# Three key and value buffers, and each round of attention scores read by two engines, in a four-layer cross-attention network

## The chip, the cores and the metric

The kernel runs on one core of one Trainium2 chip. The metric is the time on the device in microseconds (us), the median of several runs; lower is better. The input is x, 4 batches of 1024 rows of 256, with a context of 4 batches of 154 rows of 256. All data are fp32 unless a line says bf16.

## The reference, cut to what matters

Four layers follow one another. Each has a gated cross-attention of 16 heads of 16 (in layer 0 of 32 features, made by exp(z) and exp(-z)) over the 154 context rows, and then a gated feed-forward of its own kind.

```python
x = x + tanh(g_xattn[l]) * xattn_l(layernorm(x), ctx, ctx, ...)    # l = 0..3
x = x + tanh(g_ffn[l])   * ffn_l(layernorm(x), ...)

# xattn, layers 1 to 3 (layer 1 has a mask by batch, layer 3 a mask by query row and key)
scores = einsum('bhqd,bhkd->bhqk', q, k) / sqrt(16)
attn = softmax(where(mask == 0, low, scores), axis=-1)
out = einsum('bhqk,bhkd->bhqd', attn, v) @ Wo + bo
# ffn: 0 butterfly layers with gelu, 1 linear with two of eight low-rank experts,
#      2 ternary weights with gelu, 3 silu(h1) * h3 with two of eight low-rank experts
```

## The kernel before

**Streams.** Four streams (s.i from 0 to 3) each own 256 rows of a batch and go through its four layers; then they load their rows of the next batch. So there are 4 x 4 x 4 = 64 attentions and as many feed-forwards. The engines share one PSUM tensor `P` of eight banks. Banks 0 to 3 are `quad`, which holds one round of scores or of scores on their way to the exponential; banks 4 to 7 are handed out one by one.

**Keys and values.** For each batch and layer stream 0 has `key` and `val` made once for all streams. Keys land in `KB[(4b + l) % 2]`, four groups of 154 columns, and values in `VB` and `VR`. ACT's `key` waits (`s.d_o`) until all streams are through the attention two places back. POOL then scales (layer 0, L880) or masks (layer 1, L883) the keys and copies the last 26 of the 154 columns into a tile `KT` of 32 columns (L886), since the tail of 26 keys is treated apart from the first 128. After layer 2's key POOL writes the columns of ones into `VB[0]` and `VR[0]` again (`sums`), because layer 0 had overwritten them.

**One attention.** After the projection (`qp`) come four rounds, two halves of the rows (i) by two groups of heads (u). In each, `sc` on PE writes scores for 128 rows into the four banks of `quad`, 2 x 154 columns in each (L1176 in layer 0, L1192 and L1195 in layers 1 and 2, L1184 and L1188 in layer 3), and `mx` on DVE reduces all 1232 columns to eight maxima in one instruction (L1911). The next `sc` or `s2` waits for that (`quad_free`). After the fourth round POOL's `split` cuts the maxima into three bf16 parts, `mt` turns them, and the scores are computed once more with keys along the partitions and the maximum taken off: `st` (layer 0, L1222 and L1224) or `sts` (other layers, L1251 and L1254) for the tail, in two banks, and `s2` (L1275, L1278) for the first 128 keys, in `quad`. `ex` on ACT takes the exponential of 2048 columns into the tile `ET` (L1659), `pv` multiplies with the values (L1288, L1295), `no` and `nz` divide by the sums, and `out` (L1360) projects and adds.

**Order.** Each engine has a list of stages, written before the kernel is built. The generator `turns` says per stream which stage follows which. `orders` picks for each engine in turn the stream that the string `TURN` names by a digit, with costs from `parts` (nanoseconds by stage) and tokens for what is shared: one token for `quad`, one for `ET`, one for each free bank. Where it expects PE to stand for over 450 ns it writes `fill` into PE's list: matmuls on an identity (L1011) whose result nobody reads. On the chip all waits are semaphores and each engine takes its list in order.

Of the kernel before, what the change touches and what calls it, by code (L numbers as in the profile page):

```python
# [29 lines left out]
def build(nc, d, out):  # L30
# [5 lines left out]
    with ctx:  # L36
# [15 lines left out]
        zc = sb("zc", [128, 1])  # L52
# [11 lines left out]
        ctxT = [sb(f"ctx{i}", [128, 2, NP]) for i in range(2)]  # L64
# [37 lines left out]
        mk = sb("mk", [128, 4, NK], bf16)  # L102
# [8 lines left out]
        KB = [sb(f"KB{i}", [128, 4, NK]) for i in range(2)]  # L111
        KT = [sb(f"KT{i}", [128, 4, 32]) for i in range(2)]
        VB = [sb(f"VB{i}", [128, 16, 32]) for i in range(2)]
        VR = [sb(f"VR{i}", [128, 4, 32]) for i in range(2)]
# [29 lines left out]
        l_ctx = [sem(f"l_ctx{i}") for i in range(2)]  # L144
# [22 lines left out]
        g_one = sem("g_one")  # L167
# [3 lines left out]
        q_d = sem("q_d")  # L171
        q_a = sem("q_a")
# [4 lines left out]
        for i in range(NS):  # L177
# [8 lines left out]
            s.sm = sb(f"sm{i}", [128, 16, 4])  # L186
            s.g8 = sb(f"g8_{i}", [128, 6, 2, 8])
            s.mx = sb(f"mx{i}", [128, 2, 4, 4])
            s.z = sb(f"z{i}", [128, 32])
# [44 lines left out]

            s.Et = s.Et[:]
# [25 lines left out]
        def parts(name, of):  # L261
# [6 lines left out]
                  "sts": 1451 if name == "sts" and of[2] == 3 else 1113, "s2": (1105, 1105, 1105, 1540)[l],  # L268
# [4 lines left out]
                   "val": 460 if name == "val" and of[1] == 0 else 610, "norm": 885, "mx": 1357, "pv": 700, "no": 950 if l == 0 else 1240, "nz": 1655, "out": 700,  # L273
# [6 lines left out]
                   "h1": 275, "h2": 275, "norm": 985, "no": 580}  # L280
            pool = {"split": 1460 if l == 3 else 1100, "key": 2040 if name == "key" and of[1] == 0 else 1400, "mw": 1650, "norm": 1515, "sq": 960,
# [4 lines left out]
                   "key": "PA" if name == "key" and of[1:] == [0, 0] else "PAG" if name == "key"  # L286
                   else "PA", "val": "PDA" if name == "val" and of[1] == 0 else "PD", "norm": "DGA", "bias": "g",
# [11 lines left out]
        SHAPES = {"sc": "bb", "s2": "bb", "sts": "dd", "st": "ee", "lin": "bb", "tl": "hh", "val": "af", "fill": "aa"}  # L299

        def shapes(name, of):

            if name == "sts" and of[2] == 3:
                return "cd"
# [15 lines left out]
        def takes(name, of, engine):  # L320
            if (name, engine) in (("sc", "PE"), ("s2", "PE")):
                return ["quad"]
# [10 lines left out]
        def gives(name, of, engine):  # L333
            if (name, engine) in (("mx", "DVE"), ("ex", "ACT")):
                return ["quad"]
# [60 lines left out]
        def turns(s):  # L396
# [35 lines left out]
            for b in range(4):  # L432
                for l in range(4):
                    if s.i == 0:
                        if (b, l) == (0, 1):
                            yield "after", "masks"
                        if 4 * b + l >= 2:
                            for s_ in S[1:]:
                                yield "after", ("attention", s_.i, 4 * b + l - 2)
                        yield "name", "free"  # L440
# [4 lines left out]
                        yield "need", "free"  # L445
# [148 lines left out]
                "0323032023232332002022021201220221000331030331331032121212012121020321202302321203221323013213300332"  # L594
                "1310320201201203203121310310021002011321013210203231230220022013231030303311332030120121312020010320"
                "2102121313023113213200202030132321312013101003030233030232012120120103001010031303213132102112100121"
                "0231023032302000303200030030013020031000000022031032210131211111011211111112111211111330113021020230"
                "2202121023212212202222222130200222210012211032303133231232333233333333333333321230302322122032030231"
                "0321300312132330102033103021013123130100320021021321130113102032313020220220321310303033210133031201"
                "2010021200310212323121102313120103200220313221210130131003003323303020321201202101300101003130321231"  # L600
                "2130121100121021302303230003200200001000300003003000320230101230122321010031211110111111111111111113"
                "3211321202020320221210222122212222122210200222200322302310311311232323332303332333332333233333221330"
                "3221230303213031301201303312330102030201231020313100310202310213211311021230301302022022032131030303"
                "3210133031202121020031020210132312110321312010230022031222310130130110320330323023203012021101030100"
                "1303033130121120121120102120213023032300231030300031013000030000000002022030322101213011011211111111"
                "1111111112133211032102020320122102202221222012002122222222231001223123031301332312333333323333332333"
                "3332123030232212233032310103203120320331233010102030121031231031012012003023211301131020323130202202"
                "2032131030230133133032021012102003102021013232111021112330202201232030312313110103230300302232302030"
                "2101010130001130033103123112012121012102103230230230032003003030103000000032000010022100322321013121"
                "1112111111111111111112133113212232222222222222222222222332232333333333333333333333333333",  # L610
            "ACT":
                "0000300312211232020023003323101122112030103031202212201213133033103201202312231233032002021101310031"
                "3302022102102010331331213212200022021301313310323012230012100020130133020302111312201010310320223213"
                "0101023201320331000330300000021001000022313211213110111111211211211130003202012232112232222222203002"
                "2210011033132303212333333333333301202232203203102110212013230301323131123303200202313011310031303022"
                "2021102001333132112310020202230231131301033212203012100020103133020302111312201010130322202313010102"
                "3210230313033000000003100000020121321231020130110110111111111121323220221221212222222220002223030033"
                "1311212013233333303333323332312220323030110211203133013230021322131303002320231301113031030022202110"
                "2003313131212321200022023301131301302312200213010200130323021030111312101300312023022312101020212033"
# [1687 lines left out]
```

## Time and profile before

| what | value |
|---|---|
| median of 3 runs | 2433.03 us (2433.03 to 2433.96) |
| span of the profiled execution | 2431.5 us |
| time of the profiled execution beside its span | not recorded; its span is 1.5 us under the median |
| PE busy | 2331.2 us (96%), of which filler 138.0 us |
| DVE busy | 1274.5 us (52%) |
| ACT busy | 1140.6 us (47%) |
| POOL busy | 853.3 us (35%) |
| maxima, L1911 | 256 times, mean 1435 ns, 367.3 us |
| DMA | 39.28 MB, 16 GB/s on average |

Engines: PE is TensorE, DVE VectorE, ACT ScalarE, POOL GpSimd, SP SyncE, and PEld the loading of weights, which overlaps PE. An fp32 matmul stands in the trace as two records.

### The profile page before, as it was taken

To read this page: it belongs to the slowest core of one execution; us is meant where nothing else is said; L and a number is where in the kernel's file an instruction comes from. 1 tells how busy PE (TensorE), PEld (TensorE's weight loads), DVE (VectorE), ACT (ScalarE), POOL (GpSimd) and SP (SyncE) were. 2 spreads that over 40 slices of the span, in tenths; PEclk is the share of its full clock that TensorE was granted. 3 is DMA by queue.
4 is the path that set the end of the run, shared out by engine and by line. 5 is a ranking of instruction groups with operands and counts; after the bars stand their busy time and mean duration, and the time that the engine had idled before them with its cause. 6 is when DMAs were issued, how large, how long until landed. Compare 5 with 4: busy or idle time off the path is not lost.

```text
span 2431.5 us, 56000 instructions
## 1 busy us (share of the span) xinstructions
PE 2331.2 (96%) x23735; PEld 1578.7 (65%) x23735; DVE 1274.5 (52%) x2833; ACT 1140.6 (47%) x1762; POOL 853.3 (35%) x1546
## 2 busy tenths in 40 slices
PE   8999989999999999999999999899999999899999
PEld 5676545777776655577777655467777765457777
DVE  6544776545433567644442467764544346765442
ACT  5545487323345558632225546752333455683211
POOL 1232333434331333334432232334434223334342
PEclk9999999999999999999999999999999999999999
DMA  3200120000000000000000000000000000000000
GB/s 141 91 13 2 35 101 2 1 10 10 10 22 1 13 1 16 2 10 10 10 1 21 1 13 1 13 2 10 10 10 10 13 2 13 2 2 2 1 9 9
DMA packets 17462, 39.28 MB, mean 16 GB/s; under 512 B 1792, under 2 KB 11840, under 8 KB 16192
## 3 DMA queue, kind: packets, MB, share of 16 engines
q1 hardware_dynamic: 17216, 35.71, 4.3%
q8 instruction: 190, 3.11, 0.5%
q14 instruction: 56, 0.46, 0.1%
HBM read 29.78 MB, written 4.19 MB: 14 GB/s over the span
## 4 chain that ended last, share of the span: by engine, by line
PE 79%; ACT 7%; DVE 7%; issue 4%; POOL 2%; DMA 0%; ACTq 0%; POOLq 0%; DVEq 0%
PE P L1501 9%; PE P L1288 5%; PE P L1360 5%; PE P L1385 5%; PE P L1510 5%; PE P L1534 5%; PE P L1502 5%; PE P L1372 4%; PE P L1519 4%; PE P L1278 4%; ACT ET L1659 3%; PE P L1295 3%; PE P L1195 3%; PE P L1140 3%; DVE mx L1911 3%
## 5 line engine op out<-in xcount | busy, mean ns | idle before, releaser
L1911 DVE TENSOR_REDUCE mx<-P 128x8 f32<-128x1232 f32 x256 | 367.3, 1435 | 199.2 <-PE P L1195 119.9
L1501 PE MATMUL P<-Et,w 128*128 128x256 f32 x1024 | 265.4, 382 | 0.1
L1501 PEld LDWEIGHTS P<-Et,w 128*128 128x128 f32 x1024 | 191.5, 190 | 63.2 <-issue 34.5
L1955 DVE SCALAR_TENSOR_TENSOR x<-P,w_first,x 128x512 f32<-128x512 f32 x96 | 71.8, 749 | 277.6 <-PE P L1385 96.8
L1613 ACT ACTIVATE Et<-x,sm 128x256 f32<-128x256 f32 x256 | 138.7, 592 | 138.5 <-POOL sm L906 138.1
L1659 ACT ACTIVATE ET<-P 128x2048 f32<-128x2048 f32 x96 | 180.2, 1877 | 43.3 <-PE P L1278 39.9
L1737 ACT ACTIVATE gu<-P 128x256 f32<-128x256 f32 x128 | 49.1, 384 | 307.1 <-PE P L1502 290.4
L2120 DVE SCALAR_TENSOR_TENSOR gu<-gu,P 128x256 f32<-128x256 f32 x128 | 53.8, 420 | 230.0 <-ACT gu L1737 229.9
L900 POOL TENSOR_SCALAR sm<-mv 128x2 f32<-128x2 f32 x96 | 18.6, 194 | 413.5 <-DVE mv L1906 411.5
L1278 PE MATMUL P<-R,KB 32*128 32x256 f32 (+1 forms) x2560 | 155.3, 379 | 0.0
L1288 PE MATMUL P<-ET,VB 128*32 128x256 f32 x2048 | 143.4, 385 | 11.3 <-ACT ET L1659 5.3
L1502 PE MATMUL P<-gu,b 128*128 128x256 f32 x512 | 152.3, 379 | 0.0
L924 POOL TENSOR_TENSOR x<-x,w_bias 128x512 f32<-128x512 f32 x112 | 142.0, 1271 | 21.3 <-ACT Et L1613 21.1
L1011 PE MATMUL P<-identb 128*128 128x512 bf16 x507 | 138.0, 385 | 7.7 <-POOL mg L873 4.5
L953 POOL TENSOR_TENSOR R<-R 128x512 f32<-128x512 f32 x48 | 61.1, 1273 | 233.1 <-DVE R L1947 233.0
L1510 PE MATMUL P<-gu,b 128*128 128x256 f32 x512 | 134.5, 385 | 0.1
L977 POOL TENSOR_TENSOR Et<-Et,gu 128x512 f32<-128x512 f32 x48 | 61.0, 1271 | 179.0 <-DVE Et L2127 178.9
L1372 PE MATMUL P<-Et,wup 128*128 128x256 f32 x512 | 123.7, 386 | 0.0
L1534 PE MATMUL P<-w_w,R 128*128 128x256 f32 x512 | 116.4, 380 | 0.4 <-DVE R L2143 0.4
L1385 PE MATMUL P<-wdn,R 128*128 128x256 f32 x512 | 114.4, 381 | 0.0
L1510 PEld LDWEIGHTS P<-gu,b 128*128 128x128 f32 x512 | 94.1, 190 | 23.3 <-DVE gu L2127 7.7
L1372 PEld LDWEIGHTS P<-Et,wup 128*128 128x128 f32 x512 | 93.3, 190 | 24.2 <-issue 12.3
(287 smaller groups left out, 4971.3 us busy)
## 6 DMA issues: line engine op xcount, KB each, us to landing
kvw<-in_wkv SPq DMA_DIRECT2D x12, 672.0 KB, 4.1
x<-in_x SPq DMA_DIRECT2D x16, 256.0 KB, 2.7
out<-x SPq DMA_DIRECT2D x16, 256.0 KB, 2.1
w<-in_w SPq DMA_DIRECT2D x2, 1024.0 KB, 6.6
w<-in_wexp SPq DMA_DIRECT2D x1, 1028.0 KB, 9.2
w_w<-in_wcon SPq DMA_DIRECT2D x1, 1024.0 KB, 11.4
w_w<-in_m3t SPq DMA_DIRECT2D x1, 1024.0 KB, 7.2
w<-in_w1q SPq DMA_DIRECT2D x1, 1024.0 KB, 10.5
```

What stands on the lines that cost most here:

```text
L924: e.tensor_tensor(s.x[:], s.x[:], gb[:, k:k + 1, :].broadcast_to([128, 2, 256]), ALU.add).then_inc(s.g_x, 1)
L1278: t = e.matmul(quad[h, g, cols], K[G4[g], j, h], s.QT[G4[g], j if l == 0 else u, :], start=False, stop=True, skip_group_check=True)
L1288: t = e.matmul(o[G4[q], :], of(q), ET[:, g, 256 * a:256 * a + 256], start=start, stop=False, skip_group_check=True)
L1372: t = e.matmul(o[:, 256 * (j % 2):256 * (j % 2) + 256], wup[:, c, 128 * j:128 * j + 128], s.xT[:, c, :], start=c == 0, stop=c == 1)
L1385: t = e.matmul(o[:, 256 * i:256 * i + 256], s.hT[:, j, 128 * i:128 * i + 128], wdn[:, j, :], start=j == 0, stop=j == 7)
L1501: e.matmul(o, wm[:, c, js], s.xT[:, c, :], start=n == c == 0, stop=False, skip_group_check=True)
L1502: t = e.matmul(o, bm[:, js], U[:, 2 * n, :], start=False, stop=False, skip_group_check=True)
L1510: t = e.matmul(P[:, k, 256 * n:256 * n + 256], bm[:, js], U[:, 2 * n + 1, :], start=False, stop=n == 1, skip_group_check=True)
L1534: e.matmul(o, s.G[:, j, rows], w2[:, j, :], start=j == 0, stop=False)
L1613: e.activation(s.xn[:, i, :], s.x[:, i, :], ACT.Identity, bias=s.sm[:, 6, i:i + 1], scale=s.sm[:, 2, i:i + 1]).then_inc(s.a_xn, 1)
L1659: e.activation(ET[:].rearrange("p g c -> p (g c)"), quad.rearrange("p g c -> p (g c)"), ACT.Exp, bias=mb1[:, b:b + 1] if l == 1 else 0.0). ...
L1911: e.tensor_reduce(s.mx[:, i, :, 2 * u:2 * u + 2], quad[:, :, 0:2 * NK].rearrange("p g (a k) -> p g a k", a=2), AX.X, ALU.max).then_inc(q_d, 1)
```

## The change

1. Three buffers of keys instead of two (`kb`), each 160 columns wide with zeros from column 154 on, so that the tail is read from the key tile itself and `KT` goes. ACT's `key` waits for the attention three places back. Of three value buffers number 0 belongs to layer 0, the other two take turns (`vb`), so `sums` is not repeated. To make room, `ctxT` has one buffer (its next load follows layer 3's `val`), the mask of layer 1 is made for one batch at a time on POOL, and some small tiles are shared.
2. `mx` reduces banks 0 and 1 alone. A new stage `mc` on ACT copies banks 2 and 3 to SBUF (`s.half`), and `my` on DVE takes their maxima there. `quad` has two tokens, one given by `mx` and one by `mc`; `sc` and `s2` take both.
3. `sts` reads tail keys that lie apart, so its stationary tiles are 32 columns wide instead of 64, twice as many.
4. The strings `TURN` are new for all engines.

```diff
-        KB = [sb(f"KB{i}", [128, 4, NK]) for i in range(2)]
-        KT = [sb(f"KT{i}", [128, 4, 32]) for i in range(2)]
...
+        KB = [sb(f"KB{i}", [128, 4, NP]) for i in range(3)]
+        VB = [sb(f"VB{i}", [128, 16, 32]) for i in range(3)]
+        VR = [sb(f"VR{i}", [128, 4, 32]) for i in range(3)]
+
+        def kb(b, l):
+            return KB[(4 * b + l) % 3]
+
+        def vb(b, l):
+            n = 1 + (3 * b + l - 1) % 2 if l else 0
+            return VB[n], VR[n]
...
+            s.half = [w.rearrange("p (g a k) -> p g a k", g=2, a=2) for w in (R[:, 1024:1640], s.Et[:].rearrange("p a b -> p (a b)")[:, 0:616])]
...
-                        if 4 * b + l >= 2:
+                        if 4 * b + l >= 3:
                             for s_ in S[1:]:
-                                yield "after", ("attention", s_.i, 4 * b + l - 2)
+                                yield "after", ("attention", s_.i, 4 * b + l - 3)
...
                             yield "sc", s, b, l, i, u
+                            yield "name", "sc"
                             yield "mx", s, i, u
+                            yield "need", "sc"
+                            yield "mc", s, i, u
+                            yield "my", s, i, u
...
-                if l == 3 and b < 2:
+                if l == 3 and b < 3:
                     e.wait_ge(p_v0, 4 * b + 4)
-                    load_ctx(b + 2)
+                    load_ctx(b + 1)
...
-                if u == 0 and 4 * b + l >= 2:
+                if u == 0 and 4 * b + l >= 3:
                     for s in S:
-                        e.wait_ge(s.d_o, 2 * (4 * b + l - 1))
+                        e.wait_ge(s.d_o, 2 * (4 * b + l - 2))
...
+            def mc(s, i, u):
+                n = C.up(s.p_s)
+                e.wait_ge(s.p_s, n)
+                if i:
+                    e.wait_ge(d_top, tops[s.i][n - 3])
+                e.activation(s.half[u], quad[:, 2:4, 0:2 * NK].rearrange("p g (a k) -> p g a k", a=2), ACT.Copy).then_inc(q_a, 1)
...
             def mx(s, i, u):
                 e.wait_ge(s.p_s, C.up(s.p_s))
-                e.tensor_reduce(s.mx[:, i, :, 2 * u:2 * u + 2],
-                                quad[:, :, 0:2 * NK].rearrange("p g (a k) -> p g a k", a=2), AX.X, ALU.max).then_inc(q_d, 1)
-                C.up(q_d)
+                e.tensor_reduce(s.mx[:, i, 0:2, 2 * u:2 * u + 2],
+                                quad[:, 0:2, 0:2 * NK].rearrange("p g (a k) -> p g a k", a=2), AX.X, ALU.max).then_inc(q_d, 1)
+
+            def my(s, i, u):
+                e.wait_ge(q_a, copied[s.i][C.at(s.p_s) - 1])
+                e.tensor_reduce(s.mx[:, i, 2:4, 2 * u:2 * u + 2], s.half[u], AX.X, ALU.max).then_inc(d_top, 1)
```

## Rows read from the trace of the kernel before

**Rows 1.** The page: span, busy time by engine, engines of the last chain.

```profile
span 2431.5 us, 56000 instructions
PE 2331.2 (96%) x23735; PEld 1578.7 (65%) x23735; DVE 1274.5 (52%) x2833; ACT 1140.6 (47%) x1762; POOL 853.3 (35%) x1546
...
PE 79%; ACT 7%; DVE 7%; issue 4%; POOL 2%; DMA 0%; ACTq 0%; POOLq 0%; DVEq 0%
```

**Rows 2.** Windows: length, busy PE, PEld, DVE, ACT, POOL, clock, DMA; four mixed summed.

```profile
sum 912.00, PE 838.68 PEld 493.19 DVE 607.47 ACT 583.97 POOL 310.40; mean PE 209.67 PEld 123.30 DVE 151.87 ACT 145.99 POOL 77.60
...
425.60:790.40 364.80, 362.96 (x3331) 265.32 (x3328) 158.56 (x344) 132.59 (x234) 134.11 (x214) 1.00 0.03 9
...
912.00:972.80 60.80, 56.37 (x761) 30.98 (x754) 45.59 (x94) 52.31 (x66) 20.77 (x47) 1.00 0.05 16
```

**Rows 3.** Windows of filler line L1011 alone (PE, PEld): four mixed summed, start.

```profile
sum 912.00, PE 103.35 PEld 34.01; mean PE 25.84 PEld 8.50
...
0.00:60.80 60.80, 14.95 (x52) 5.46 (x53) 0.97 0.38 141
```

**Rows 4.** Waits of PE: us in total, times, longest.

```profile
PE P L1195 <- ACT ET L1659: 6.8, 17, 0.9
PE P L1184 <- DVE mx L1911: 6.7, 17, 0.8
PE P L1288 <- ACT ET L1659: 5.3, 9, 2.0
PE P L1288 <- issue: 4.7, 14, 0.5
...
PE P L1275 <- DVE mx L1911: 3.8, 10, 0.6
...
PE P L1195 <- DVE mx L1911: 3.5, 8, 0.6
...
PE P L1176 <- ACT ET L1659: 1.6, 4, 0.6
```

**Rows 5.** Timeline of a layer-3 attention: start, us, what.

```profile
951.24 0.70 PE L1188 MATMUL P<-KB,R 32*64 32x308 f32 x16
...
952.13 1.43 DVE L1911 TENSOR_REDUCE mx<-P 128x8 f32<-128x1232 f32 x1
...
953.62 0.31 PE L1184 MATMUL P<-mb,identb 32*64 32x308 bf16 x1 [0.27 <-DVE mx L1911]
```

**Rows 6.** Groups by line: busy us, mean ns, idle before; maxima and tail matmuls.

```profile
L1911 DVE TENSOR_REDUCE mx<-P 128x8 f32<-128x1232 f32 x256 | 367.3, 1435 | 199.2 <-PE P L1195 119.9
...
L1254 PE MATMUL P<-R,KT 32*64 32x256 f32 x768 | 56.0, 379 | 0.0
...
L1251 PE MATMUL P<-R,selt 32*64 32x256 bf16 x384 | 28.3, 280 | 3.7 <-ACT R L1640 2.5 <-issue 0.8 <-ACT R L1679 0.2
...
L1224 PE MATMUL P<-R,KT 32*32 32x256 f32 x512 | 20.3, 376 | 0.0
...
L1222 PE MATMUL P<-R,selt 32*32 32x256 bf16 x256 | 9.5, 273 | 0.8 <-ACT R L1640 0.8
```

**Rows 7.** Nearest reduction and ACT copies from PSUM; the third row by source.

```profile
L2038 DVE TENSOR_REDUCE sm<-Et 128x2 f32<-128x512 f32 x16 | 10.9, 682 | 22.8 <-ACT Et L1613 22.7
...
L1622 ACT ACTIVATE Et<-P 128x512 f32<-128x512 f32 x96 | 56.9, 595 | 97.6 <-PE P L1116 97.3
...
L1667 ACT ACTIVATE R<-P x49: 360/384/600, 56.0 to 1942.8; 128x256 f32<-128x256 f32 x34, 128x512 f32<-128x512 f32 x15
```

**Rows 8.** Windows of L1911 alone, first and last of the four mixed stretches.

```profile
182.40:425.60 243.20, 51.38 (x36) 1.00 0.11 35
...
2006.40:2188.80 182.40, 39.49 (x28) 0.99 0.02 5
```

**Rows 9.** Waits of ACT: keys.

```profile
ACT KB L1595 <- PE P L1084: 1.3, 2, 1.1
```

**Rows 10.** DMA issues: KB each, median us to landing.

```profile
ctx<-in_ctx SPq DMA_DIRECT2D x4, 160.0 KB, 3.9
```

More of the change, by code:

```diff
@@ L62, in res @@
             return W[name]
-        ctxT = [sb(f"ctx{i}", [128, 2, NP]) for i in range(2)]
+        ctxT = sb("ctxT", [128, 2, NP])
         first = res("first", [128, 467])
@@ L143, in build @@
         l_last = sem("l_last")
-        l_ctx = [sem(f"l_ctx{i}") for i in range(2)]
+        l_ctx = sem("l_ctx")
         FIRST = ("first",)
@@ L333, in gives @@
         def gives(name, of, engine):
-            if (name, engine) in (("mx", "DVE"), ("ex", "ACT")):
-                return ["quad"]
+            if (name, engine) in (("mx", "DVE"), ("mc", "ACT"), ("ex", "ACT")):
+                return ["quad"] * (2 if name == "ex" else 1)
             if (name, engine) == ("pv", "PE"):
@@ L444, in turns @@
                         yield "name", "key"
-                        yield "need", "free"
+                        yield "need", "begun"
+                        if 3 * b + l >= 3:
+                            n = 3 * b + l - 3
+                            before = 4 * (n // 3) + n % 3 + 1 if l else 4 * (b - 1)
+                            for s_ in S[1:]:
+                                yield "after", ("attention", s_.i, before)
                         yield "val", b, l
@@ L599, in build @@
[L599 to L603, printed above, removed]
@@ L762, in build @@
         ORDER = orders()
+        tops = [[n for n, of in enumerate((of for of in ORDER["DVE"] if of[0] == "my"), 1) if of[1] is s] for s in S]
+        copied = [[n for n, of in enumerate((of for of in ORDER["PE"] if of[0] in ("sc", "s2")), 1)
+                   if of[0] == "sc" and of[1] is s] for s in S]
         def sp_program(e):
@@ L929, in split @@
                 parts_ = s.MX.rearrange("p i (g r) -> p (i g) r", r=32)
-                e.wait_ge(q_d, [n for n, of in enumerate((of for of in ORDER["DVE"] if of[0] == "mx"), 1)
-                                if of[1] is s][16 * b + 4 * l + 3])
+                e.wait_ge(d_top, tops[s.i][16 * b + 4 * l + 3])
                 e.wait_ge(s.g_z, C.at(s.g_z))
@@ L1248, in sts @@
                 for u in range(2):
-                    o = [banks[g // 2][64 * h:64 * h + 64, 256 * u:256 * u + 256] for g, h in enumerate((0, 1, 1, 0))]
-                    for g in range(4):
-                        e.matmul(o[g], selt[G4[g], 2 * u:2 * u + 2, :].rearrange("p a k -> p (a k)"), s.MT[G4[g], :],
-                                 start=l < 3 and u == 0, stop=False, skip_group_check=True)
-                    for g in range(4):
-                        t = e.matmul(o[g], K[G4[g], u, :], s.QT[G4[g], u, :], start=False, stop=True, skip_group_check=True)
+                    eight = [(g, a, banks[g // 2][G4[2 * h + a], 256 * u:256 * u + 256]) for a in range(2)
+                             for g, h in enumerate((0, 1, 1, 0))]
+                    for g, a, o in eight:
+                        e.matmul(o, selt[G4[g], 2 * u + a, :], s.MT[G4[g], :], start=l < 3 and u == 0, stop=False,
+                                 skip_group_check=True)
+                    for g, a, o in eight:
+                        t = e.matmul(o, K[G4[g], 2 * u + a, :], s.QT[G4[g], u, :], start=False, stop=True,
+                                     skip_group_check=True)
                 t.then_inc(s.p_q, 1)
```

209 lines of the change are left out of this document (101 added, 108 removed).

## Prediction

> **What bounds the kernel now.** I read the page first. TensorE is busy for 96% of the span and carries 79% of the chain that ended last [rows 1]. This kernel's planner also writes filler matmuls into TensorE's list wherever it expects a gap, so that busy share is not all work. The windows view by stage and the same view for the filler line L1011 alone part the two. The span alternates between two kinds of stretch. In the dense ones (the last feed-forward, line L1501 and its kin) PE is busy 362.96 of 364.8 us with almost no filler, so nothing that shortens a wait can help there. The four mixed ones, with over half of the attention rounds in them (182.4 to 425.6, 790.4 to 1033.6, 1398.4 to 1641.6 and 2006.4 to 2188.8 us), sum to 912.0 us. PE is busy 838.7 us there and 103.4 of these are filler [rows 2, 3]. So idle 73.3 + filler 103.4 = 176.7 us is what a better order could win there. About 30 to 40 us more lie at the start (14.95 of filler in the first 60.8 us) and at the end, and the change hardly touches those.
>
> Next, what ends PE's waits. PE idles 2431.5 - 2331.2 = 100.3 us in all. The maxima (L1911) end 6.7 + 3.8 + 3.5 = 14.0 us of it, 14%, in 35 waits of 0.40 us on average, the longest 0.8. The exponentials (L1659) end 6.8 + 5.3 + 1.6 = 13.7 us of it, also 14% [rows 4]. The timeline of one layer-3 attention shows why: the last score matmul ends at 951.94, DVE begins its maxima at 952.13, holds all four banks of `quad` for 1.43 us, and the next round starts at 953.61 [rows 5]. One round occupies `quad` for about 2.66 us, and more than half of it is DVE's.
>
> **The change part by part, on the profiled execution's span of 2431.5 us.**
>
> The hold of `quad`. The maxima took 1435 ns for 1232 elements, and DVE's reduction of 512 took 682 [rows 6, 7]. The slope is 753 / 720 = 1.05 ns per element, so 616 elements cost 682 + 109 = 0.79 us. On ACT 512 elements cost 595 ns and 256 a median of 384, so a copy of 616 costs 0.68 us [rows 7]. Both run side by side after one handover, so the hold falls by 1435 - 790 = 0.645 us in each of the 256 rounds. The mixed stretches hold 36 + 35 + 37 + 28 = 136 rounds (the first and the last of the four windows are shown) [rows 8], and of them only what PE waited for counts. Filler hides waits in the same places, so I give the maxima their 14% of the whole 176.7 us: 24.7 us. As the mean wait (0.40) is under 0.645, most of it can go, though another wait may come last in its stead. Bounds 0 and -25 us; I take four fifths, **-20**.
>
> The length of one attention. Each attention has four rounds. The first three release `quad` 0.645 sooner, 1.9 us. The fourth now ends later for `split`, which waits for the maxima of the copied half: the two reductions in a row are at least 1.58 us and copy, handover (0.19) and reduction are 0.68 + 0.19 + 0.79 = 1.66, against 1.44, so +0.2. Net -1.7 us; a stream has 16 attentions, 27 us if its chain set the time everywhere. 136 of 256 rounds, 53%, lie in the mixed stretches: 14 us. Here the new lists belong too. They can spend the shorter hold, and the third buffer lets a key run three attentions ahead of the slowest stream instead of two. ACT's keys hardly ever waited for an old buffer: the 1.3 us they idled was for PE [rows 9]. So I give the buffer nothing by itself. Bounds 0 and -50 (a third of the 176.7 us less the first term); I take **-14**.
>
> `sts`. The tail's stationary tiles become 32 wide, so matmuls double from 16 to 32 instructions (records from 24 to 48, as an fp32 matmul has two). Before, layers 1 to 3 cost (56.0 + 28.3) / 48 = 1.76 us of PE per call, and layer 0, which already has the 32-wide form, (20.3 + 9.5) / 16 = 1.86 [rows 6]. So twice the instructions cost 0.1 us and not twice the time: 48 x 0.1 = **+5**. Bounds +3 and, if equal moving data from one row group went one after the other, 48 x 0.6 = +29; the row of layer 0 is so near in form that I stay by it. In layer 3 the form of tile now also differs from that of `s2` right behind, 16 more switches. The nearest row is PE's idle without a releaser ahead of the 128 x 32 matmuls, 4.7 / 14 = 0.34 us [rows 4]; 0 to +5, I take **+2**. The Trainium skill (TensorEngine Tiling (Array Packing), Tiling Modes, Key Properties) says that changing the tiling mode drains TensorE; by that rule a switch costs something each time. No row of this case isolates one, and without a cost the sum would be 2 us lower.
>
> ACT and DVE. The copies are 256 x 0.68 = 174 us more on ACT (1140.6 to 1315). In the mixed stretches 136 x 0.68 = 92 us come on top of 584.0, which makes 74% of 912. An ACT queue 16% fuller brings the exponentials later. Their 14% of 176.7 us is 24 us, times 0.16 is 4 us. Behind a waiting copy also stand the turns and projections of other streams, so I take **+7**. Lower bound 0. The upper one is read in the fullest window, 912.0 to 972.8 us: ACT 52.3 busy, with 8 rounds, so 8 x 0.68 = 5.4 more gives 57.7 of 60.8 us. If ACT were the limit in such a window in each of the four mixed stretches, that is +22. On DVE two halves cost 1.58 against 1.435, 256 x 0.145 = 37 us, of which 20 in the mixed stretches (607.5 to 627, 69%) [rows 2]. That is covered by the third of the time in which DVE stands idle there; without that cover it would cost the same 20 us. The Trainium skill (VectorE: DVE Perf Modes, the section on the TRN2 errata) speaks against cutting the reduction: each instruction pays a fixed cost, 120 cycles from PSUM and 58 from SBUF. An estimate by its table is 0.77 + 0.70 us for the halves against 1.41, some 16 us in all; the rows say 37, and neither is on the path.
>
> At nothing: the 16 copies to `KT` go from POOL (35% busy) and one mask per batch comes there; masking keys for layer 1 alone stays. One buffer for `ctx`: its load now begins after layer 3's `val` and takes 3.9 us [rows 10]. Layer 0's keys of the next batch come with a whole attention between, so it is hidden; uncovered it would be 3 x 3.9 = 12 us. SP stands in order, so it could sit behind a `store`, which is waited for anyway.
>
> The sum: -20 - 14 + 5 + 2 + 7 = -20, so 2411.5 us of span. The profiled span is 1.5 us under the median of the three runs (2433.03), so **2413 us**.
>
> **Rivals.**
> The lists win much more (21%). The planner's order was tied to one token for `quad`; with two halves and three buffers the dense feed-forward of one stream may lie beside the attention of others. For it: 176.7 us of slack stand in stretches where neither DVE (67%) nor ACT (64%) is full. Against it: ACT reaches 86% in some windows, and the digits of the new PE list show the same long runs of one stream in the last feed-forward. Time: all 24.7 us of the maxima, a fifth of the other 152 (30), less 14: 2433 - 41 = 2392, or down to 2375 with a third.
>
> Nothing is left (14%). `quad` is freed sooner, but the next wait is one of the other 86%, and the two gains shrink to the 14 us of cost: 2433 us. For it: the waits for the maxima are short, and PE usually has other streams' matmuls between the rounds. This also stands for the change not doing what it says.
>
> ACT becomes the limit, slower (20%). A round needs both readers, and ACT takes its list in order. A copy that stands behind an exponential of 1.88 us, or behind a table load, gives the banks back later than the old reduction did. It decides once copies come more than 1.435 - 0.68 = 0.75 us late on average. For it: ACT 95% full in the window above. Against: the lists know of the copy and place it. Price: +22 in the four full windows, +7 for `sts`, +7 of queueing elsewhere, less some 20 still won: 2433 + 16 = 2449.
>
> The forecast has 45%, with a range of its own from 2401 to 2427.
>
> **The numbers.** The measurement of this kernel tells about 0.2% (4.9 us) from no change. Faster by more: 45% + 21% + 2% of the third case = 68%. Within 0.2%: 12%. Slower: 20%. The range for 8 in 10 goes from 2378, which leaves some 5% of the large-gain case below, to 2446, which leaves about 12% above.
>
> **What the profile will show.** The maxima should have two groups of 256 at about 0.79 us, and a new ACT copy 256 times at 0.68. PE's waits for the maxima should fall from 14.0 us to under 5, some of them named after the copy. Filler and idle in the mixed stretches should go from 177 to about 150 us. The tail matmuls should cost 1.86 us a call, ACT some 1315 us and DVE 1311. The prediction fails if copies start long after the scores end, if filler stays at 138 us, or if the new lists shift so much that the mixed stretches are no longer the same ones. It also fails if the granted clock, 1.00 in most windows, falls in longer gaps.

## The result, and the profile after

The changed kernel takes 2415.53 us, the median of four runs (2414.88 to 2420.39), beside 2433.03 for the kernel before. The ratio is 0.9931, with a 95% interval from 0.9917 to 0.9945. So 17.5 us are gone, where 20 had been forecast.

The page of the profile first: the span, and the busy time of each engine. It answers to [rows 1].

```profile
span 2413.9 us, 58830 instructions
...
PE 2317.5 (96%) x24838; PEld 1578.3 (65%) x24838; DVE 1292.7 (54%) x3088; ACT 1303.3 (54%) x2026; POOL 845.0 (35%) x1522
```

ACT is busy 162.7 us longer and DVE 18.2, and PE 13.7 us less, although its tail has twice the instructions. Most of that is filler, which fell from 138.0 to 126.3 us (507 matmuls to 458). PE's idle time went from 100.3 to 2413.9 - 2317.5 = 96.4. What PE does beside filler is 2191.2 us, against 2193.2 before. Nearly the whole gain is therefore slack in PE's list, that is, idle time and filler: 238.3 us before, 222.7 after, 15.6 of the 17.6 us between the two spans. The groups of the page, by line (busy us, mean ns, idle before them and what ended most of it):

```profile
L1926 DVE TENSOR_REDUCE mx<-P 128x4 f32<-128x616 f32 x256 | 203.1, 793 | 188.5 <-PE P L1208 97.6
...
L1024 PE MATMUL P<-identb 128*128 128x512 bf16 x458 | 126.3, 390 | 15.6 <-POOL mg L895 5.6
...
L1668 ACT ACTIVATE Et<-P 128x616 f32<-128x616 f32 x128 | 87.2, 681 | 88.0 <-PE P L1208 43.9
L1668 ACT ACTIVATE R<-P 128x616 f32<-128x616 f32 x128 | 87.1, 681 | 70.3 <-PE P L1208 33.4
```

and from the same kind of groups, asked for by engine, the reductions of the copied half and the tail matmuls, which answer to [rows 6]:

```profile
L1931 DVE TENSOR_REDUCE mx<-R 128x4 f32<-128x616 f32 x128 | 100.4, 784 | 6.4 <-ACT R L1668 6.4
L1931 DVE TENSOR_REDUCE mx<-Et 128x4 f32<-128x616 f32 x128 | 100.2, 784 | 7.4 <-ACT Et L1668 7.3
...
L1265 PE MATMUL P<-R,KB 32*32 32x256 f32 x1536 | 61.7, 376 | 0.0
...
L1262 PE MATMUL P<-R,selt 32*32 32x256 bf16 x768 | 30.5, 272 | 5.0 <-ACT R L1649 4.7 <-issue 0.3
```

One reduction of 1435 ns has become one of 793 ns from PSUM and one of 784 ns from SBUF, with a copy of 681 ns on ACT beside them. These durations may not simply be added up, because one instruction starts before the one in front of it ends. Two reductions back to back in DVE's timeline (start, length, what):

```profile
943.24 0.79 DVE L1926 TENSOR_REDUCE mx<-P 128x4 f32<-128x616 f32 x1
943.94 0.79 DVE L1931 TENSOR_REDUCE mx<-Et 128x4 f32<-128x616 f32 x1
```

The second starts 0.70 us after the first, which takes 0.79. So the durations of the halves exceed those of the whole reduction by 203.1 + 200.6 - 367.3 = 36.4 us, but DVE's busy time, which counts overlap once, grows by far less: by 14.4 us against the run below that differs from the changed kernel in the halves alone (1278.3 to 1292.7).

By stage, the same four mixed stretches (slices of equal share of the span, 905.25 us in all), every engine first, then filler line L1024 alone; they answer to [rows 2, 3]:

```profile
sum 905.25, PE 838.15 PEld 506.74 DVE 599.62 ACT 623.14 POOL 300.90; mean PE 209.54 PEld 126.68 DVE 149.91 ACT 155.78 POOL 75.22
```

```profile
sum 905.25, PE 94.39 PEld 31.49; mean PE 23.60 PEld 7.87
```

Idle 67.1 and filler 94.4 make 161.5 us, where it was 176.7: 15.2 of the 17.5 us were won in the mixed stretches. The waits of PE (us in total, times, longest), which answer to [rows 4], look quite different from that:

```profile
PE P L1208 <- ACT ET L1675: 6.3, 11, 1.0
...
PE P L1197 <- DMA mbTs<-mbT: 4.7, 1, 4.7
PE P L1300 <- ACT ET L1675: 4.6, 11, 1.3
...
PE P L1024 <- DVE mx L1926: 3.9, 4, 1.6
PE P L1197 <- DVE mx L1926: 3.6, 8, 1.1
...
PE P L1208 <- DVE mx L1926: 2.8, 7, 0.9
...
PE P L1287 <- DVE mx L1926: 1.3, 4, 0.5
...
PE P L1205 <- DVE mx L1926: 1.0, 3, 0.4
...
PE P L1189 <- DVE mx L1926: 0.6, 2, 0.3
```

Maxima still end 3.9 + 3.6 + 2.8 + 1.3 + 1.0 + 0.6 = 13.2 us of PE's idle time (9.3 if those ahead of filler are left aside), hardly less than the 14.0 before; waits under the name of the copy itself (L1668) add 3.0. Whoever looked only here would say that the change had done nothing. The row `mbTs<-mbT` is new: one single wait of 4.7 us. Layer 3's first masked scores wait there for the last of the transfers that spread the mask over the partitions. In the kernel before, the last of them was issued at 305.3 us and the first scores that need it ran at 360.9; in the changed kernel it was issued at 352.4, and PE stood until 354.6. The same wait stands in the runs below that use these lists (4.0 us even with the buffers of the kernel before), so it came with the new order. The prediction has no term for it. Part of the reason for the 13.2 shows in the timeline of a late copy (start, length, what; idle before and releaser in brackets):

```profile
938.21 2.11 PE L1024 MATMUL P<-identb 128*128 128x512 bf16 x9
...
938.39 1.91 ACT L1719 ACTIVATE R<-R 128x2048 f32<-128x2048 f32 x1
...
939.17 0.79 DVE L1926 TENSOR_REDUCE mx<-P 128x4 f32<-128x616 f32 x1
940.21 0.67 ACT L1668 ACTIVATE R<-P 128x616 f32<-128x616 f32 x1
...
940.94 0.10 PEld L1197 LDWEIGHTS P<-mb,identb 32*64 32x64 bf16 x1 [1.12 <-DVE mx L1926]
940.97 0.29 PE L1197 MATMUL P<-mb,identb 32*64 32x308 bf16 x1 [0.66 <-issue]
```

DVE is through with its half at 939.96. The copy stood behind another stream's instruction of 1.91 us, ended only at 940.88, and then the next round began, at 940.94 with its weight load. The banks were held until 940.88 by ACT, 0.9 us longer than by DVE; without the split DVE would have given them back at 939.17 + 1.43 = 940.60. The bracket books the 1.12 us before that weight load to DVE's maxima, so some waits under that name are the copy's. In the timeline I paired the ends of all 256 copies and reductions: the copy ends first or within 0.1 us of the reduction in 206 rounds, more than 0.1 us later in 50, more than 0.5 us later in 31, at worst 2.8 us. What these delays add to the holds is 39 us in all, of which only a part meets a waiting PE.

One more thing moved with the slack: the clock that PE was granted. Its mean is 0.997 in the profile before and 0.999 after, of a full clock of 2.4 GHz, and the windows show why. These are the stretches at the lower of its two levels, half of it; first the four of the kernel before, then the one of the changed kernel (stretch, length, PE busy, clock, DMA share, GB/s):

```profile
38.91:42.33 3.42, 3.42 (x21) 0.50 0.00 0
1414.49:1417.90 3.41, 3.41 (x40) 0.50 0.00 0
1537.37:1540.78 3.41, 3.41 (x30) 0.50 0.03 7
2086.91:2090.32 3.41, 3.41 (x22) 0.50 0.00 0
```

```profile
352.08:358.91 6.83, 4.32 (x39) 0.50 0.78 279
```

In the 6.8 us ahead of them PE had stood idle for 1.4 to 3.0 us in the kernel before, and for 2.2 us in the changed one, whose stretch begins within the wait for the mask. If what PE did in them took twice as long as at the full clock, they cost 13.65 / 2 = 6.8 us before and 4.32 / 2 = 2.2 after. The runs say much the same: of the four of the changed kernel, three with a mean clock of 0.999 took about 2415 us and the one with 0.996 took 2420.4, so 0.002 is worth some 3.4 us. An estimate of 3 to 5 of the 17.5 us is therefore the clock. No run holds it fixed, so it can't be told apart from the shorter idle times that go with it.

### The profile page after: what moved, and what is told of

It reads as the page before. It is cut to its first block and busy times, and to the rows that moved or that the text cites. A ratio compares the mean times of both kernels' runs of the same rounds, so it can differ in the third digit from the quotient of the medians.

```text
span 2413.9 us, 58830 instructions
## 1 busy us (share of the span) xinstructions
PE 2317.5 (96%) x24838; PEld 1578.3 (65%) x24838; DVE 1292.7 (54%) x3088; ACT 1303.3 (54%) x2026; POOL 845.0 (35%) x1522
## 5 line engine op out<-in xcount | busy, mean ns | idle before, releaser
L1926 DVE TENSOR_REDUCE mx<-P 128x4 f32<-128x616 f32 x256 | 203.1, 793 | 188.5 <-PE P L1208 97.6
L938 POOL TENSOR_TENSOR x<-x,w_bias 128x512 f32<-128x512 f32 x112 | 142.2, 1273 | 11.7 <-ACT Et L1622 11.6
L1024 PE MATMUL P<-identb 128*128 128x512 bf16 x458 | 126.3, 390 | 15.6 <-POOL mg L895 5.6
L1668 ACT ACTIVATE Et<-P 128x616 f32<-128x616 f32 x128 | 87.2, 681 | 88.0 <-PE P L1208 43.9
L1668 ACT ACTIVATE R<-P 128x616 f32<-128x616 f32 x128 | 87.1, 681 | 70.3 <-PE P L1208 33.4
```

What stands on the lines that cost most here:

```text
L938: e.tensor_tensor(s.x[:], s.x[:], gb[:, k:k + 1, :].broadcast_to([128, 2, 256]), ALU.add).then_inc(s.g_x, 1)
L1668: e.activation(s.half[u], quad[:, 2:4, 0:2 * NK].rearrange("p g (a k) -> p g a k", a=2), ACT.Copy).then_inc(q_a, 1)
L1926: e.tensor_reduce(s.mx[:, i, 0:2, 2 * u:2 * u + 2], quad[:, 0:2, 0:2 * NK].rearrange("p g (a k) -> p g a k", a=2), AX.X, ALU.max).then_inc ...
```

## The experiments

Two theories went in. **A**: the shorter hold of `quad` (with lists made for it) brings the gain, the copies cost a little of it, and the third key buffer nothing. **B**: the gain comes from elsewhere, from the third buffer or from lists that are simply better searched, and the copy is free or does harm. Experiments that put new stages or a longer search to use have their own written-out lists. Filler is not in these lists; the generator places it anew for every kernel, so its amount may differ where the stages' order is the same. The twelve runs were made in three groups of four, each with its own runs of the kernel before (medians 2433.03, 2433.68 and 2433.14 us). Each ratio is taken within its group, and a difference in us between runs of different groups is no finer than about 1 us.

**The shorter hold undone.** The changed kernel and its lists, without the stages `mc` and `my`; one reduction takes all four banks again.

```
-    yield "mc", s, i, u
-    yield "my", s, i, u
...
-    e.tensor_reduce(s.mx[:, i, 0:2, 2 * u:2 * u + 2], quad[:, 0:2, 0:2 * NK]...)
+    e.tensor_reduce(s.mx[:, i, :, 2 * u:2 * u + 2], quad[:, :, 0:2 * NK]...)
```

> The changed kernel with its new lists, but one reduction of all four banks again: the ACT copies and the reductions from SBUF are taken out of the lists, every other stage stays in its order. Theory (the shorter hold of the banks, which the new lists are cut to, brings the gain): 2433 to 2442 us, that is 18 us or more above the changed kernel, and PE's waits for the maxima at 14 us or more. Rival (the new lists or the three buffers bring it, whoever reads the scores): 2412 to 2420 us, since ACT then has 174 us less to do.

Measured: 2443.54 us, ratio 1.0043 (1.0029 to 1.0058). That is 28 us above the changed kernel and 10 above the kernel before, and 1.5 above the expected range. The page, and its waits of PE:

```profile
PE 2324.4 (95%) x24836; PEld 1580.5 (65%) x24865; DVE 1278.3 (52%) x2831; ACT 1149.9 (47%) x1768; POOL 846.6 (35%) x1522
```

```profile
PE P L1279 <- DVE mx L1918: 9.2, 23, 1.2
PE P L1190 <- DVE mx L1918: 7.5, 14, 1.1
PE P L1201 <- DVE mx L1918: 7.3, 14, 1.6
...
PE P L1198 <- DVE mx L1918: 3.6, 7, 0.9
...
PE P L1272 <- DVE mx L1918: 1.4, 3, 0.6
PE P L1182 <- DVE mx L1918: 1.4, 4, 0.5
```

With the same lists and a hold of 1436 ns, the waits for maxima are 30.4 us; with 793 ns they are 13.2. Here the row does show what the hold costs, since the order is the same. Idle and filler together are 115.6 + 133.0 = 248.6 us against 222.7, so 25.9 of the 26.1 us between the two spans are slack. (Of it 6.7 us are filler that the generator placed on top, 485 matmuls against 458.) The 28 us are what the shorter hold brings after the copies and DVE's second reduction have been paid. B's part about the lists falls: the new lists without the shorter hold are worse than the old ones. They spend it, and by themselves they lose. (Of the 10 us some 4 belong to the tail and the other parts, as is shown further down, so the order itself is about 6 us worse.)

**Two key buffers.** The changed kernel with `KB` two deep, the waits set back to the attention two before.

```
-            return KB[(4 * b + l) % 3]
+            return KB[(4 * b + l) % 2]
```

> The changed kernel with its new lists, but keys in two buffers by turns, and the key stage of ACT waits for the attention two places back again. Theory (the third key buffer by itself brings nothing, because ACT hardly ever waited for an old one): 2413 to 2418 us, the same as the changed kernel. Rival (the new lists use the room of three): 2420 us or more, with idle time of ACT or PE in front of the keys.

Measured: 2415.98 us, ratio 0.9935 (0.9918 to 0.9951), against 0.9931 with three. The third key buffer brings nothing that can be measured, as the theory had it.

**The 32-wide tail in the kernel before.** Only `sts` is changed, the lists stay.

```
+    eight = [(g, a, banks[g // 2][G4[2 * h + a], 256 * u:256 * u + 256]) for a in range(2) for g, h in enumerate((0, 1, 1, 0))]
-    for g in range(4):
-        t = e.matmul(o[g], K[G4[g], u, :], s.QT[G4[g], u, :], ...)
+    for g, a, o in eight:
+        t = e.matmul(o, K[G4[g], 2 * u + a, :], s.QT[G4[g], u, :], ...)
```

> The kernel before with one edit: the tail scores of layers 1 to 3 use stationary tiles of 32 columns, twice as many matmuls. Theory (0.1 us more a call, 48 calls, most of it on the path): 2438 us, and up to 2443 if the switch of tile form in layer 3 costs as well; the tail lines at 1.86 us a call. Rival (PE fills its gaps elsewhere, so a longer call hides in idle and filler time): 2431 to 2435 us. If equal moving data went one after the other: 2460 us.

Measured: 2435.56 us, ratio 1.0011 (1.0002 to 1.0021): 2.5 us slower, with an interval from 0.5 to 5.1. That is between the rival's range (up to 2435) and the theory's 2438. The groups of its tail:

```profile
L1255 PE MATMUL P<-R,KT 32*32 32x256 f32 x1536 | 61.2, 376 | 0.0
...
L1252 PE MATMUL P<-R,selt 32*32 32x256 bf16 x768 | 29.3, 273 | 3.5 <-ACT R L1642 2.3 <-issue 0.8 <-ACT R L1681 0.2
```

That is 90.5 / 48 = 1.89 us a call against 1.76, 6.2 us more busy time in all, of which 2.5 us reach the span. The rest ran where there would have been slack.

**Twice the copy.** Two key buffers (to make room in SBUF), and behind each `mc` a second ACT copy of 616 elements, from a constant to a scrap tile that nobody reads. The lists know nothing of it.

```
+    e.activation(idle[:].rearrange("p (a k) -> p a k", a=7), ones[:, 0:88].unsqueeze(1).broadcast_to([128, 7, 88]), ACT.Copy)
```

> The changed kernel, keys in two buffers to make room, and behind each of the 256 copies ACT makes one more of the same size between tiles that nobody else uses, after the banks are given back: 174 us more on ACT (about 1478 us in all), nothing else moved. Theory (ACT's load costs by queueing, about 7 us for the first 174): 7 to 22 us above the changed kernel, 2423 to 2438 us. Rival (ACT has room and its load costs nothing): 2413 to 2419 us. Rival (ACT is about to become the limit in the mixed stretches, where it is at 77%): 2445 us or more.

Measured: 2448.58 us, ratio 1.0065 (1.0048 to 1.0081), 32.6 us above the kernel with two key buffers.

```profile
PE 2320.2 (95%) x24809; PEld 1576.1 (64%) x24838; DVE 1294.4 (53%) x3088; ACT 1452.9 (59%) x2282; POOL 847.9 (35%) x1522
...
L1675 ACT ACTIVATE idle<-ones 128x616 f32<-128x616 f32 x256 | 182.5, 713 | 0.0
```

The added copies last 182.5 us, but they overlap the copies in front of them, and ACT's busy time rose by 149.4 us (from 1303.5 with two key buffers). On an ACT that was 54% busy these cost 32.6 us of span, 0.22 us for each. It was not free at half load. The theory (7 to 22 us) was too low, and the time lies in the range of the second rival (2445 or more). That ACT is about to become the limit isn't shown by it: the lists did not know of these copies, and ACT is at 59%.

**The halves alone.** The kernel before (two buffers, `KT`, 64-wide tail, two buffers of `ctx`), with `mx`, `mc`, `my` and the changed kernel's lists; only POOL's has eight stages more.

```
 kernel before
-    mx: reduce quad[:, 0:4]                (1 stage, holds quad)
+    mx: reduce quad[:, 0:2]; mc: copy quad[:, 2:4] to s.half[u]; my: reduce s.half[u]
```

> The kernel before with its own buffers (two for keys and values, KT, two for ctx) and its own 64-wide tail tiles, and only the halves of the change: mx, mc and my, with the new kernel's lists (POOL's extra key stages put where they can first start). Theory after the first four runs (halves together with lists cut to them are the whole gain, buffers are nothing): 2412 to 2419 us. Rival (the three value buffers, the zero-padded keys or the single ctx buffer carry a part): 2421 us or more.

Measured: 2411.28 us, ratio 0.9905 (0.9888 to 0.9921). The halves with their lists gain 21.8 us by themselves. Everything else of the change together (third key buffer, value buffers, the masks, `KT` gone, the 32-wide tail, one `ctx`) takes back 4.2, which is not quite what the two intervals can tell apart (up to 0.9921 and from 0.9917).

**The old design, lists searched on.** The kernel before with only its written-out lists replaced.

> The kernel before with no edit but its lists, which were searched further from where they stood. Theory (the halves are needed, order alone gives little): 2422 us or more, that is at most 11 us under the kernel before. Rival (searching the lists anew is what pays, whoever reads the scores): 2418 us or less, near the changed kernel.

Measured: 2428.4 us, ratio 0.9977 (0.9968 to 0.9987). A better order alone, as far as this search found one, is worth 4.6 us. That is what remains of B.

**The changed kernel, lists searched on.**

> The changed kernel with no edit but its lists, searched further for the same time as in the run of the kernel before with its lists searched on. Theory (the new lists are near what this search finds, and the distance between the two designs stays over 10 us): 2408 to 2414 us. Rival (the changed kernel's order is spent): 2414 to 2418 us. Rival (an order that only looks better): 2418 or more.

Measured: 2413.89 us, ratio 0.9919 (0.9902 to 0.9935): 1.6 us less than as given, less than the intervals can tell. Its order was not held back by a lack of search of this kind.

**Twice the reduction.** The changed kernel with one more DVE reduction of 616 elements, from a constant, behind each `my`; the lists know nothing of it.

```
+    e.tensor_reduce(idle[:], ones[:, 0:88].unsqueeze(1).broadcast_to([128, 7, 88]), AX.X, ALU.max)
```

> The changed kernel, and behind each of the 256 reductions from SBUF DVE makes one more of the same size (0.79 us) from and to tiles that nobody else uses: about 200 us more on DVE (1493), nothing else moved. It answers the run in which ACT's copy was doubled (33 us for 182 us of ACT). Theory (each in-order queue that carries a stream's next step costs by its load, DVE as ACT): 20 to 40 us above the changed kernel, 2435 to 2455 us. Rival (DVE has room, as the forecast had it): 2415 to 2422 us. Rival (DVE is nearer its limit than ACT): 2460 or more.

Measured: 2465.04 us, ratio 1.0129 (1.0112 to 1.0146), 49.5 us above the changed kernel.

```profile
PE 2330.7 (95%) x24838; PEld 1579.5 (64%) x24838; DVE 1462.1 (59%) x3344; ACT 1306.8 (53%) x2026; POOL 846.8 (34%) x1522
...
L1937 DVE TENSOR_REDUCE idle<-ones 128x7 f32<-128x616 f32 x256 | 200.4, 783 | 0.0
```

Here too the added reductions overlap those in front: they last 200.4 us, and DVE's busy time rose by 169.4. That is 0.29 us of span for each us, at 54% busy before and 59% with it. The time is above the theory's range and in that of the rival who had DVE nearer its limit than ACT (2460 or more). Part of it is the clock: all four runs have a mean of 0.994. In the profile PE spent six stretches at half clock, 27.3 us:

```profile
sum 27.31, PE 24.92; mean PE 4.15
```

By the same working as above they cost 12.5 us, against 2.2 in the changed kernel, so some 10 of the 49.5 us are an effect of the gaps through the clock. By the ratio of 0.29 the 14.4 us that the halves add to DVE's busy time cost 4 us. That is an estimate, and from above, since the lists of the change do place `my`.

**No copy.** The changed kernel without `mc`: `quad` is given back by `mx`, `my` reduces a constant of the same size, and so the maxima of half of the heads are left out (the exponentials are scaled by 0.001). DVE's work stays as it is, but `my` has no copy to wait for; ACT's 174 us of copies go, and `quad` has one reader.

```
-    yield "mc", s, i, u
...
-    e.wait_ge(q_a, copied[s.i][C.at(s.p_s) - 1])
-    e.tensor_reduce(s.mx[:, i, 2:4, 2 * u:2 * u + 2], s.half[u], AX.X, ALU.max)
+    e.tensor_reduce(s.mx[:, i, 2:4, 2 * u:2 * u + 2], ones[...].broadcast_to([128, 2, 2, NK]), AX.X, ALU.max)
```

> The changed kernel without ACT's copies. Banks 2 and 3 are given back by mx, which reads banks 0 and 1 alone; my makes a reduction of the same size (616 elements) from a constant tile, so the true maxima of half the heads are left out, and the exponentials scale their input by 0.001 to stay finite. DVE's load and the hold of the banks by DVE stay, 174 us of ACT go. Theory (ACT's load costs 33 us per 182 us, as the doubled copy showed, also for the first copy): about 2384 us. Rival (the lists had placed the copies where ACT had room, so the first costs less than one more that no list knows): 2395 to 2410 us. Forecast's term for ACT (7 us): 2408.

Measured: 2403.8 us, ratio 0.9878 (0.9862 to 0.9895). The copies, placed by the lists as they are, cost 11.7 us, what `my` waits for them included. That is 0.08 us for each us of ACT's busy time (1303.3 to 1147.9), and it is the rival's case. Against the whole reduction in the same lists (2443.54) this kernel is 39.7 us faster: so much is the shorter hold worth in this order before the copies are paid, with DVE's second reduction in it. Its groups show the same reduction from PSUM as the changed kernel, and less filler, 118.7 us against 126.3 (the generator placed 436 matmuls instead of 458):

```profile
L1921 DVE TENSOR_REDUCE mx<-P 128x4 f32<-128x616 f32 x256 | 203.0, 793 | 193.6 <-PE P L1204 98.1
...
L1020 PE MATMUL P<-identb 128*128 128x512 bf16 x436 | 118.7, 387 | 11.3 <-POOL mg L891 5.6
```

**The halves alone, lists searched on.** The kernel of 2411.28 us with a longer search.

> The kernel of the run with the halves alone (buffers and tail of the kernel before), its lists searched on. Theory (halves in the old buffers need fewer matmuls for the tail, and the lists were not cut to them yet): 2399 to 2408 us. Rival (its order was spent): 2409 to 2413 us.

Measured: 2409.16 us, ratio 0.9900 (0.9884 to 0.9917). Only 2 us more; I had expected about 2399 to 2408, and the rival's range (2409 to 2413) holds. Against the old design searched on (2428.4) it is 19.2 us faster, so the gain of the halves holds when both sides have had their search.

**Halves in three of the four layers.** The kernel of 2411.28 us, but layer 2 keeps the single reduction (a stage `mq`) and makes no copy; first with the lists as they were, the lost stages struck out.

```
+    HALF = (0, 1, 3)
...
+    mq: e.tensor_reduce(s.mx[:, i, :, 2 * u:2 * u + 2], quad[:, :, 0:2 * NK]..., AX.X, ALU.max)     (layer 2)
     mx, mc, my as above                                                                             (layers 0, 1, 3)
```

> As the run with the halves alone, but in layer 2 one reduction takes all four banks again and ACT copies nothing there; the lists are the same less the stages that go. It asks which layers the halves pay in. Theory (their gain is the shorter hold less ACT's and DVE's load, and in layer 2's rounds the two are about even): 2409 to 2417 us, within 6 us of the run with the halves alone (2411.3). Rival (every layer's rounds gain alike, a quarter of 28 us): 2418 us or more.

Measured: 2412.42 us, ratio 0.9917 (0.9900 to 0.9933), against 2411.28 (0.9905) with halves everywhere. In layer 2 the 64 copies and 64 extra reductions cost as much as the shorter hold gives, as far as these intervals can tell, and the rival (2418 or more) is excluded.

**The same with lists searched on.**

> The same kernel with its lists searched on. It should be the fastest: 43 us of ACT and 9 us of DVE less than with halves in all layers, in lists that can use it. Theory: 2392 to 2402 us. Rival (layer 2 gains as the others do, once the lists are searched): no better than the halves in all layers with lists searched on.

Measured: 2402.06 us (2399.09 to 2403.08), ratio 0.9869 (0.9853 to 0.9886). This is the best version that keeps the whole computation: 31 us under the kernel before and 13.5 under the changed one, in intervals that lie apart. Against the halves in all layers searched on (2409.16) it is 7.1 us faster, and there the intervals still touch (up to 0.9886 and from 0.9884). Groups of its page:

```profile
L1948 DVE TENSOR_REDUCE mx<-P 128x4 f32<-128x616 f32 x192 | 152.1, 792 | 153.3 <-PE P L1220 72.3
...
L1036 PE MATMUL P<-identb 128*128 128x512 bf16 x424 | 116.7, 387 | 7.8 <-POOL mg L896 4.6
```

Filler is at 116.7 us and PE idle for 2400.3 - 2306.5 = 93.8, 210.5 us of slack against 222.7. ACT is busy 1263.3 us, 40 less than in the changed kernel.

## Why the prediction was right, and where its terms were not

**The net result** came from the forecast's own case: -17.5 measured, -20 forecast, well in its range from 2401 to 2427. The halves gained less than their terms (-20 - 14 + 7 = -27 forecast, -21.8 measured with the halves alone) and the rest of the change cost less (+7 forecast, +4.2 measured). The two errors have opposite signs, so the sum is better than its parts, which is luck. Some 3 to 5 us of the gain also went with PE's clock, for which the forecast had no term.

**The hold and the new lists (-20 and -14).** The mechanism was right: in one and the same order of stages, the hold of 1436 instead of 793 ns costs 28 us with the copies paid and 39.7 without them, and this stands in idle time and filler. The size of the gain before its costs can be put together: 21.8 net, 11.7 for the copies (measured in the changed kernel), and for DVE's extra work something between 0.08 and 0.29 us for each of its 14.4, that is 1 to 4. This makes 35 to 38 us, an estimate, against 34 forecast. The split of it between a first term for the wait and a second one for the length of an attention can't be measured, because an order spends the shorter hold as it likes. It stays an argument. What the shorter hold gives in the old order wasn't run.

**ACT's copies (+7).** Under-sized: 11.7 us. The lower bound of nothing is excluded, the upper of 22 is not reached. The step priced queueing ahead of the exponentials; what it left to a rival is the lateness of the copy itself, which 50 of 256 rounds show. That rival ("ACT becomes the limit") named a mechanism that is there, but not its case: it asked for copies 0.75 us late on average, and here 203 of 256 end before DVE's reduction does, while 50 are late. How the 11.7 us divide between late copies, queueing and the waits of `my` was not measured.

**DVE at nothing.** The reason given for this term failed. I had called 20 us of reductions in the mixed stretches covered by DVE's idle third. The doubled reduction shows 0.29 us of span for each us on a DVE that is 54% busy, so the idle third is no cover for work that the lists do not place. That a late `my` is late for `split`, and what stands behind it on DVE is late too, is my explanation; no run takes it apart. The load was mis-sized as well: 37 us adds up durations, and the busy time rose by 14.4. With 1 to 4 us by the estimate above, nothing was not far off in size. The Trainium skill (VectorE: DVE Perf Modes, the TRN2 errata) has 58 cycles of fixed cost for a source in SBUF and 120 for one in PSUM, by which (an estimate) the halves would take 0.70 and 0.77 us. It adds that its row for VectorE is too low for the duration of one operation from SBUF, with about 150 cycles measured, which would give 0.80. The rows have durations of 784 and 793 ns, so the 150 cycles fit better and the source makes 9 ns of difference, not 65. The 0.70 us fit the distance from one start to the next, as in the two rows at 943.24 and 943.94. The skill's 16 us for cutting the reduction, which the prediction set against its own 37, is close to the 14.4 that DVE's busy time shows.

**`sts` (+5, and +2 for switching).** The busy time was forecast well: 1.86 us a call, measured 1.89 in the old lists and 1.92 in the new ones. The span took 2.5 of it (0.5 to 5.1), against 7 forecast with the switches, since part of the 6 us more ran in what had been slack. This 2.5 us holds the switch of form as well, so no separate price for switching is visible; it was measured in the old lists alone. The high bound of 29 us, one row group after the other, is excluded; its 0.6 us a call had been worked out from no row.

**At nothing: the third buffer, `ctx`, the masks.** The third key buffer is measured at nothing (0.9935 against 0.9931). The load of `ctx`, `ctxT<-in_ctx` in the list of DMA issues, takes 4.0 us and shows up in no wait of PE; the transfer that does is that of layer 3's mask, 4.7 us, which the new order brought. All parts outside the halves make 4.2 us, and the tail 2.5 of it. The other 1.7 us were not taken apart, and can't be told from none.

**What the profile was to show.** The two groups at 0.79 us and the copy at 0.68 came as said. ACT came to 1303.3 us instead of 1315 and DVE to 1292.7 instead of 1311, because the forecast added up durations that overlap. The granted clock did not fall on the whole: its mean went from 0.997 to 0.999. Slack in the mixed stretches went to 161.5 instead of 150. The forecast of PE's waits for the maxima, from 14.0 to under 5, was wrong: they are 13.2. The mistake was to read that row as a quantity of its own. In a fixed order it follows the hold (30.4 to 13.2); from one order to another it told nothing here, presumably because the new order starts rounds so much closer that they wait again. It also isn't all DVE's: with the copies gone it is still 12.0 us, and the timeline shows waits under that name that ended with the copy.

**What stays open.** A longer search gave 10 us with halves in three layers and 2 us with halves in four. Whether layer 2 without halves leaves an order more freedom, or the search was luckier there, can't be told from one search of each. The DVE share is an estimate and was not measured by itself. Nor was the clock's share, and nobody tried to issue layer 3's mask transfers earlier, though the 4.7 us in front of them are the one wait that the new lists added.

## What to carry to other kernels

In a kernel that pads its bound engine with filler, read slack as idle plus filler by stage, and not from the waits named after one instruction; that row compares kernels only if their order is the same. Give added work on an in-order engine a price even at half load: here it was 0.22 us (ACT) and 0.29 us (DVE) of span per us of busy time where the order did not know of it, and 0.08 (ACT) where it was placed. Take the load from busy time and not from added durations, since neighbours overlap. Splitting a reader so that a bank comes free sooner is worth trying layer by layer, and every such change has to be judged with an order made for it: without the shorter hold the new lists were some 6 us worse than the old ones, and with it the kernel was 17.5 us faster, or 21.8 with the halves alone. After a new order, look through all waits of the bound engine for one that was not there before, such as the one for the mask here, and compare the granted clock.

## What the runs showed of the hardware

A reduction of 616 fp32 elements takes DVE 784 ns from SBUF and 793 from PSUM, so moving the source to SBUF does not make it cheaper. Back to back, the next one starts after 0.70 us. On ACT a copy of 616 takes 681 ns from PSUM, and one of 616 from an SBUF constant (88 elements read seven times) 713, so SBUF is not the cheaper side there either. A call of the tail with 32 matmuls on 32 x 32 tiles costs only 0.13 to 0.16 us more than one with 16 on 32 x 64 (1.89 and 1.92 against 1.76 us), though each instruction is as long as before (376 ns against 379). TensorE's clock fell to half for 13.65 us in all before and for 6.83 us after; two kernels 17 us apart can differ by 3 to 5 us through it (an estimate).
